# Second attention: its first half prepared inside the low-rank network, its projections made as 64-row products side by side in two banks

## The reference

```python
def _L0_ffn_ref(x, U1, V1, b1, U2, V2, b2):
    P = jnp.einsum('bsd,dr->bsr', x, U1)
    H = jax.nn.gelu(jnp.einsum('bsr,rf->bsf', P, V1) + b1)
    Q = jnp.einsum('bsf,fr->bsr', H, U2)
    return jnp.einsum('bsr,rd->bsd', Q, V2) + b2

def _L1_attn_ref(x, Wqkv, bqkv, Wr, br):
    xh = x.reshape(b, c, h, he).transpose(0, 2, 1, 3)        # 16 heads of 16
    qkv = jnp.einsum('bhce,ef->bhcf', xh, Wqkv) + bqkv       # one 16 x 48 weight for all heads
    q, k, v = jnp.split(qkv, 3, axis=-1)
    att = jnp.einsum('bhqe,bhke->bhqk', q, k) / jnp.sqrt(jnp.float32(he))
    mask = jnp.tril(jnp.ones((c, c), dtype=att.dtype), k=-1)
    att = jax.nn.softmax(att * mask, axis=-1)
    out = jnp.einsum('bhqk,bhke->bhqe', att, v)
    return out.transpose(0, 2, 1, 3).reshape(b, c, d) @ Wr + br
```

## Time and profile before

| | us |
|---|---|
| Median of 3 runs | 2801.05 |
| Lowest, highest | 2794.32, 2802.73 |
| Profiled execution | 2797.78 |
| its span, first to last instruction | 2796.0 |

### The profile page before, as it was taken

One profiled execution on the slowest core, in us unless ns is written; L12 is line 12 of the kernel. 1 busy time (PEld: TensorE's weight loads), 2 busy tenths in 40 slices (PEclk: granted clock), 3 DMA queues, 4 the chain that ended last, 5 costly groups with the idle time before them and its releaser, 6 DMA issues. The chain is left out here.

```text
span 2796.0 us, 75274 instructions
## 1 busy us (share of the span) xinstructions
PE 2615.3 (94%) x27044; PEld 1818.8 (65%) x27044; DVE 2280.6 (82%) x6931; ACT 2078.2 (74%) x3782; POOL 1811.9 (65%) x3152
## 2 busy tenths in 40 slices
PE   5999999999999999997889789999999999699999
PEld 3677777777777777775333257777777777466766
DVE  5999999999999999986655468888888888488998
ACT  4998899999998999895333257667677776478886
POOL 3767666777667766774421157677777767588885
PEclk8999999999999999999899889999999999899999
DMA  4334433444334433441000166655556664000001
GB/s 116 68 62 77 79 61 62 74 80 79 61 64 80 73 61 62 72 72 47 10 0 1 32 106 105 105 96 104 97 101 97 104 99 71 1 16 24 24 24 39
DMA packets 110387, 182.21 MB, mean 65 GB/s; under 512 B 27008, under 2 KB 96384, under 8 KB 97920
## 3 DMA queue, kind: packets, MB, share of 16 engines
q1 hardware_dynamic: 106560, 176.61, 34.7%
q10 hardware_dynamic: 3456, 0.79, 0.2%
HBM read 116.25 MB, written 60.29 MB: 63 GB/s over the span
## 5 line engine op out<-in xcount | busy, mean ns | idle before, releaser
L808 POOL TENSOR_TENSOR ratio_scores<-ratio_scores,ratio_max_cols 128x512 f32<-128x512 f32 (+3 forms) x1024 | 726.1, 726 | 319.3 <-DVE ratio_max_cols L718 316.9
L1328 DVE CUSTOM_DVE_ANT_0 zeroed_unused<-bank,zeroed_drop 128x512 bf16<-128x512 f32 (+3 forms) x1024 | 440.0, 484 | 121.1 <-PE bank L198 120.9
L198 PE MATMUL bank<-ratio_k_stack,ratio_q_stack 102*128 102x512 bf16 (+7 forms) x2048 | 506.3, 303 | 33.4 <-DVE ratio_max_cols L718 17.5
L718 DVE CUSTOM_DVE_ANT_0 ratio_scores<-bank,ratio_scores 128x512 f32<-128x512 f32 (+3 forms) x1024 | 472.4, 489 | 22.2
L1216 ACT ACTIVATE zeroed_prob<-bank 128x512 f32<-128x512 f32 x640 | 370.1, 593 | 161.2 <-PE bank L1103 160.3
L580 ACT ACTIVATE ratio_prob<-bank 128x512 f32<-128x512 f32 x640 | 378.4, 592 | 105.5 <-PE bank L494 102.7
L708 DVE TENSOR_TENSOR ratio_scores<-bank,ratio_inverse 128x512 f32<-128x512 f32 x640 | 435.9, 681 | 16.8 <-PE bank L198 9.6
L491 PE MATMUL bank<-const_f_sb,ratio_scores 128*128 128x128 f32 x2560 | 409.9, 274 | 0.9 <-ACT ratio_prob L580 0.9
L569 ACT ACTIVATE ratio_inverse<-bank 128x512 f32<-128x512 f32 x640 | 381.1, 596 | 12.7 <-PE bank L201 12.6
L573 ACT ACTIVATE ratio_inverse<-ratio_inverse 128x1024 f32<-128x1024 f32 x320 | 338.6, 1058 | 10.1
L1446 POOL TENSOR_SCALAR_AFFINE_SELECT zeroed_prob<-zeroed_prob 128x256 f32<-128x256 f32 (+1 forms) x640 | 227.7, 361 | 178.0 <-ACT zeroed_prob L1216 172.2
(11 more groups left out here) (178 smaller groups left out, 5412.6 us busy)
## 6 DMA issues: line engine op xcount, KB each, us to landing
ratio_q_stack<-ratio_parts_q SPq DMA_DIRECT2D x186, 128.0 KB
ratio_k_stack<-ratio_parts_k SPq DMA_DIRECT2D x186, 128.0 KB
zeroed_q_stack<-zeroed_parts_q SPq DMA_DIRECT2D x186, 128.0 KB, 4.7
zeroed_k_stack<-zeroed_parts_k SPq DMA_DIRECT2D x186, 128.0 KB, 7.7
ratio_parts_q<-ratio_parts SPq DMA_DIRECT2D x96, 128.0 KB
ratio_parts_k<-ratio_parts SPq DMA_DIRECT2D x96, 128.0 KB
zeroed_parts_q<-zeroed_parts SPq DMA_DIRECT2D x96, 128.0 KB
zeroed_parts_k<-zeroed_parts SPq DMA_DIRECT2D x96, 128.0 KB
```

The costliest lines, as they stand in the source:

```text
L198: i = e.matmul(bank[:, off:off + w], qs[0:rows, s, hh, ib * P:(ib + 1) * P], ks[0:rows, s, hh, 0:w], start=(k == 0), stop=mask is None, sk ...
L718: i = e.tensor_tensor_reduce(seg, dot_banks[n % 2][:, at], seg, 1.0, 0.0, ALU.mult, ALU.max, mx[:, pair % M_BUFS, c:c + 1])
L808: i = e.tensor_tensor(seg, seg, mx[:, pair % M_BUFS, c:c + 1].to_broadcast([P, w]), ALU.subtract)
L1328: i = e.tensor_tensor_reduce(unused[:, n % 2, at], bank[:, at], drop[:, L - (ib + 1) * P:L], 1.0, 0.0, ALU.add, ALU.max, mx[:, pair % FOLD ...
```

## The change

The first half's preparation (half 0) moves into rows 10 to 14 of the low-rank network (`START_AT`, `START_XN`, `START_MEMSETS`), with its constants and its gathers; what the stages share is now allocated around both (`ZeroedStart`), and the ternary weights' work tiles lie in the stacks' memory. ACT takes the Ln and Exp of the layer norm there, between two Gelus. Half 1 is prepared from slots 0 and 2.

A projection is now four products of 64 rows and 64 columns: heads 0 to 3 in `prep_bank`, heads 4 to 7 in `o_bank` (in the low-rank network in `post_bank`), the two halves of the 512 positions one below the other. ACT and DVE read each bank with an instruction of its own. So a projection waits until ACT has copied the last group out of `o_bank`, and every attend waits until the projections before it are read (`two_banks`). Values likewise: eight products for four. q and k are projected in slots 13 and 16; all three later steps follow one, two and three slots behind; the attends stand at 10, 12, 13 instead of 9, 11, 13, that is in slots 18, 20, 21 and 8, 10, 11. A side's parts are written by 6 DMAs with pieces of 256 elements (512 bytes) instead of 3 with 512.

```diff
 FOLD_PROBS = 12
-Z_ATTEND_AT = (9, 11, 13)
+Z_ATTEND_AT = (10, 12, 13)
...
-Z_ROOT_AT, Z_XN_AT, Z_TURN_AT, Z_VALUES_AT, Z_SUFFIX_AT = 0, (3, 6), (6, 9), 3, 19
-Z_SPLIT_AT, Z_REST_AT, Z_MID_AT, Z_LO_AT = (11, 15), (12, 16), (13, 17), (14, 18)
+Z_ROOT_AT, Z_XN_AT, Z_TURN_AT, Z_VALUES_AT, Z_SUFFIX_AT, Z_SPLIT_AT = 0, (3, 6), (6, 9), 3, 19, (13, 16)
+Z_REST_LAG, Z_MID_LAG, Z_LO_LAG = 1, 2, 3
+QUARTER = HALF // 2
 GROUPS_FROM, ROW_STEPS = ZEROED_LAG + 18, (71, 81, 91, 101)
-
-Z_SECOND_AT, Z_SECOND_REST_AT, Z_SECOND_MID_AT, Z_SECOND_LO_AT = (1, 5), (2, 6), (3, 7), (4, 8)
...
+def split_at(n, halves):
+
+    half, at = divmod(n, HALF_UNITS)
+    if n in Z_SECOND_AT:
+        return 1, Z_SECOND_AT.index(n)
+    if half >= 0 and at in Z_SPLIT_AT and half + 2 < halves:
+        return half + 2, Z_SPLIT_AT.index(at)
     return None, None
 
...
-            def project(half, side):
+            def project(half, side, n):
+
                 q.wait_ge(w.sem, w.loaded)
                 q.wait_ge(s["prep_read"], prep[sides[side], half] - 1)
-                e.matmul(prep_bank[:, :], w.w_in[:, side, :], xnT[:, half % 2, :], start=True, stop=True).then_inc(s["prep_filled"])
-
-            def values(half):
+                q.wait_ge(s["o_group"], groups_before(n))
+                for bank, heads in quarters:
+                    for k in range(2):
+                        i = e.matmul(bank[k * 64:(k + 1) * 64, 0:L // 2], w.w_in[heads, side, heads],
+                                     xnT[heads, half % 2, k * L // 2:(k + 1) * L // 2], start=True, stop=True, skip_group_check=True)
+                i.then_inc(s["prep_filled"])
+
+            def values(half, n):
                 q.wait_ge(s["prep_read"], prep["v", half] - 1)
+                q.wait_ge(s["o_group"], groups_before(n))
                 for t in range(T):
-                    i = e.matmul(prep_bank[:, t * P:(t + 1) * P], xnT[:, half % 2, t * P:(t + 1) * P], w.w_in[:, 2, :],
-                                 start=True, stop=True)
+                    for bank, heads in quarters:
+                        i = e.matmul(bank[:, t * 64:(t + 1) * 64], xnT[heads, half % 2, t * P:(t + 1) * P], w.w_in[heads, 2, heads],
+                                     start=True, stop=True, skip_group_check=True)
                 i.then_inc(s["prep_filled"])
 
...
                     q.wait_ge(s["prep_read"], prep["v", g // 2])
                     q.wait_ge(s["o_group"], g)
+                    q.wait_ge(s["prep_read"], two_banks(n))
                     attend(e, g, part, o_bank, values_ones, prob, FOLD_PROBS, STACKS).then_inc(s["attended"])
...
-                q.wait_ge(s[f"parts_{sides[side]}"], 48 * half)
-                e.activation(parts[:, side, 0, :], prep_bank[:, :], ACT.Identity, bias=w.bias_qk[:, side:side + 1]).then_inc(s["hi"])
+                q.wait_ge(s[f"parts_{sides[side]}"], 96 * half)
+                for k, (bank, _) in enumerate(quarters):
+                    i = e.activation(parts[:, side, 0, k * L // 2:(k + 1) * L // 2], bank[:, 0:L // 2], ACT.Identity,
+                                     bias=w.bias_qk[:, side:side + 1])
+                i.then_inc(s["hi"])
 
...
+                split_half, side = split_at(n, halves)
+                if split_half is not None:
+                    split(split_half, side)
+                split_half, side = split_at(n - Z_MID_LAG, halves)
+                if split_half is not None:
+                    second_part(split_half, side)
...
-                e.scalar_tensor_tensor(out=rest[:, :], in0=prep_bank[:, :], scalar=w.bias_qk[:, side:side + 1],
-                                       in1=parts[:, side, 0, :], op0=ALU.add, op1=ALU.subtract).then_inc(s["prep_read"])
+                for k, (bank, _) in enumerate(quarters):
+                    cols = slice(k * L // 2, (k + 1) * L // 2)
+                    i = e.scalar_tensor_tensor(out=rest[:, cols], in0=bank[:, 0:L // 2], scalar=w.bias_qk[:, side:side + 1],
+                                               in1=parts[:, side, 0, cols], op0=ALU.add, op1=ALU.subtract)
+                i.then_inc(s["prep_read"])
...
-                                parts[:, side, part, :]).then_inc(s[f"parts_{sides[side]}"], 16)
+                    for k in range(2):
+                        to = part_dram[side][half % 2][part][:, :, k * L // 2:(k + 1) * L // 2]
+                        e.dma_start(to.rearrange("d (m h) t -> h d m t", m=2),
+                                    parts[k * 64:(k + 1) * 64, side, part, :]).then_inc(s[f"parts_{sides[side]}"], 16)
...
+
+    slot = lambda b, f: b * FC + f
+    START_ROOT, START_XN = slot(11, 0), (slot(11, 5), slot(12, 4))
+    START_AT = dict(zip(START_STEPS, (slot(11, 7), slot(12, 7), slot(13, 1), slot(13, 7), slot(14, 1), slot(14, 7))))
+    START_TAILS = slot(14, 4)
+    START_MEMSETS = slot(10, 5), slot(11, 1), slot(11, 5), slot(11, 7), slot(12, 1), slot(12, 5)
...
-        w_pos = sb("ternary_w_positive", [P, 2, n_w])
-        w_neg = sb("ternary_w_negative", [P, 2, n_w])
+
+        flat = lambda stack: stack[:, :, :, :].rearrange("p s h t -> p (s h t)").bitcast(F32)
+        w_loaded = flat(start.qs)[:, 0:2 * n_w].rearrange("p (k n) -> p k n", k=2)
+        w_pos = flat(start.ks)[:, 0:2 * n_w].rearrange("p (k n) -> p k n", k=2)
+        w_neg = [flat(stack)[:, 2 * n_w:3 * n_w] for stack in (start.qs, start.ks)]
...
+            def start_project(side, n):
+
+                q.wait_ge(zeroed.sem, zeroed.loaded)
+                q.wait_ge(s["prep_read"], prep[sides[side], 0] - 1)
+                q.wait_ge(s["post_read"], post((n - OUT_AT[1] - 1) // FC - 1, 1))
+                for bank, heads in quarters:
+                    for k in range(2):
+                        i = e.matmul(bank[k * 64:(k + 1) * 64, 0:L // 2], zeroed.w_in[heads, side, heads],
+                                     start.xnT[heads, 0, k * L // 2:(k + 1) * L // 2], start=True, stop=True, skip_group_check=True)
+                i.then_inc(s["prep_filled"])
...
+                q.wait_ge(s["prep_read"], two_banks(slot(b + 1, OUT_AT[pair])))
...
+            def start_root():
+                e.preload_act_table_set("natural_log_exp_and_others")
+                e.activation(net.rstd[:, 0:T], net.mean_var[:, 0:T, 1], ACT.Ln, bias=net.eps_ln[:, :]).then_inc(zs["log_var"])
+                q.wait_ge(zs["log_var"], 1)
+                e.activation(net.rstd[:, 0:T], net.rstd[:, 0:T], ACT.Exp, scale=-0.5).then_inc(zs["rstd"])
+
...
+                if late[0] in ("q", "k"):
+                    side = side_of(late[0])
+                    q.wait_ge(zs["hi"], side + 1)
+                    q.wait_ge(zs["lo"], side)
+                    for k, (bank, _) in enumerate(quarters):
+                        cols = slice(k * L // 2, (k + 1) * L // 2)
+                        i = e.scalar_tensor_tensor(out=start.rest[:, cols], in0=bank[:, 0:L // 2], scalar=zeroed.bias_qk[:, side:side + 1],
+                                                   in1=start.parts[:, side, 0, cols], op0=ALU.add, op1=ALU.subtract)
...
+                q.wait_ge(zs["hi"], side + 1)
+                q.wait_ge(zs["lo"], side + 1)
+                for part in range(3):
+                    for k in range(2):
+                        to = start.part_dram[side][0][part][:, :, k * L // 2:(k + 1) * L // 2]
+                        e.dma_start(to.rearrange("d (m h) t -> h d m t", m=2),
+                                    start.parts[k * 64:(k + 1) * 64, side, part, :]).then_inc(zs[f"parts_{sides[side]}"], 16)
+            for heads, sem in ((slice(0, GROUP), zs["gathered_first"]), (slice(GROUP, HALF), zs["gathered0"])):
```

More of the change, by code:

```diff
@@ L1015, in zeroed_attention @@
+def zeroed_attention(net, w, start):
     nc, B, L, D, T = net.nc, net.B, net.L, net.D, net.T
@@ L1358, in prepare @@
                     values(half + 1)
-                if half == 0 and at in Z_SECOND_REST_AT:
-                    split(1, Z_SECOND_REST_AT.index(at))
                 if half % 2 == 0 and half + 2 < halves:
@@ L1377, in dve @@
                     maxima(n)
+                split_half, side = split_at(n - Z_REST_LAG, halves)
+                if split_half is not None:
+                    split(split_half, side)
                 if half < halves:
@@ L1470, in pool @@
                     split_maxima(pair - 1)
+                split_half, side = split_at(n - Z_LO_LAG, halves)
+                if split_half is not None:
+                    split(split_half, side)
                 if half < halves:
```

268 lines of the change are left out of this document (177 added, 91 removed).

## The result

| | us |
|---|---|
| Before, median of 4 runs | 2798.77 (2794.32 to 2802.73) |
| After, median of 4 runs | 2924.86 (2922.58 to 2931.66) |
| Ratio | 1.0455, 95% interval 1.043 to 1.048 |
| Profiled execution after | 2923.84, span 2922.1 |

The change costs 126 us. The forecast was 2845, 44 us over the 2801.05 that it started from, with a range of its own of 2825 to 2865. The direction and the mechanism came, the size did not.

What follows compares the result with a forecast made beforehand. PE was taken to bound the steady part, with DVE just hidden behind it. 2797.8 - 25 (start) + 70 (steady halves) = 2842.8 us, forecast as 2845 since the runs' median lies 3.3 above that execution; range 2825 to 2865.

Steps and rivals of the forecast that it cites:

- The start: Half 0's preparation inside the low-rank network and half 1's after it: -25 us, bounds -20 and -34.
- The mechanism: Steady half: PE waits 2.2 us before attend 0 for DVE's rest of k, which waits for POOL's low part of q.
- The size of the half, +2.4 us: Net cost of each steady half, paid in halves 1 to 29: 29 x 2.4 = +70 us.
- Attend 0 starts at S+8.2: Slot 18, S being the half's dots(12): attend 0 starts at S+8.2, not S+5.1; dots(19) comes 2.7 us later.
- Values: taken 0: Eight products for four in v's projection: between half of 0.95 us and twice, taken as 0.
- Slots 2 to 12: -0.3: These slots lose q's projection: worth nothing in halves with a turn of x, about 0.6 us otherwise, mean -0.3.
- The clock, taken as 1.00: PE's clock in the steady halves: the forecast added no cost for a slower clock behind the 2.2 us wait.
- rival C: PE's clock slows behind waits from about 3 us on, some 2 us more per half: 2900 us, chance 0.06.
- my own sign: Listed as showing the forecast wrong: PE's clock below 1.00 between 1650 and 2400.
- Transfers: 0: Writes and gathers of k's parts in steady halves: cost 0, some 3 us of cover stay; without it 1 to 3.
- Rivals A: POOL less behind; DVE's own work alone sets attend 0 at S+7.1, +38 us: 2814 us, chance 0.22.
- B: No wait at attend 0; PE saves 2 x 0.4 us per half, -23: 2753 us, chance 0.14.

Runs made afterwards that it cites:

- Experiment 1: Changed kernel's start only; later halves project q, k and v as before the change, attends at 9, 11, 13: 2776.22 us, ratio 0.9919 to the kernel before.
- experiment 3: Changed kernel with a second place for k's rest from half 2 on: 2855.00 us, ratio 1.0199 to the kernel before.
- experiment 10: Experiment 1 with v alone made as in the changed kernel, eight products of 64 rows in two banks: 2786.64 us, ratio 0.9951 to the kernel before.
- experiment 2: Experiment 1 (one bank) with the changed kernel's late slots, attends at 10, 12, 13 and projections at 13 and 16: 2834.69 us, ratio 1.0123.
- experiments 5: Changed kernel with q's low part ahead of the split of the maxima on POOL in slot 16: 2892.50 us, ratio 1.0324 to the kernel before.
- 7: Changed kernel with both a second place for k's rest and q's low part ahead of the split of the maxima: 2898.54 us, ratio 1.0349.
- Experiment 4: Changed kernel with the first block of shifted products made 34 times over ahead of attend 0 in slot 18: 2897.48 us, ratio 1.0345.
- experiment 8: Second place for k's rest and q's low part ahead of the maxima split, plus 18 repeated products ahead of attend 0: 2875.91 us, ratio 1.0270.

## Why the prediction was right or wrong

**The start: -25, measured -23.** Its steps held: the network grew by 5.0 us (I had 6, bounds 4 to 10), dots(0) came at 1581.7 (1582.6), dots(20) at 1615.6 (1614). Experiment 1 shows that it stands by itself.

**The mechanism: right.** One PE gap per half ahead of attend 0, released by DVE's rest of k, which waited for POOL's low part of q. The wait was forecast as 2.2 us and is mostly 2.4. That the two are so near is in part luck: PE comes to attend 0 at S+6.7 where I had 6.0, and DVE lets it go at S+9.1 where I had 8.2, so both ends were wrong the same way. The trace agrees with the page "TensorEngine Tiling (Array Packing)" of the Trainium skill, section PSUM Bottleneck, that the emptying of PSUM may become the bottleneck: in experiment 3, with POOL out of the chain, attend 0 still waits 1.1 us for the engine that empties the banks.

**The size of the half, +2.4 us: the step that failed.** At full clock a half costs 3.66 more (27.14 and 28.67, mean 27.90, against the 24.24 of 23.69 and 24.79), so 29 x 3.66 = 106 instead of 70. Two terms were mis-sized and make up nearly all of the 1.26 a half:
- "Attend 0 starts at S+8.2": S+9.1, and so 16.6 us from dots(12) to dots(22) where I had 15.7, 0.9 too little. q's projection waits for ACT's copy of the group and starts at S+1.0, not 0.7; its middle part stands behind two exponentials and ends at S+4.5, not 3.95; the split of the maxima takes 1.5 us, not 1.34, and begins when the mask of slot 15 ends, S+5.3, where I had 4.8. I added up durations and took each queue as free at the right moment.
- "Values: taken 0": 0.28 a half, by experiment 10.

"Slots 2 to 12: -0.3" was nearly right for what it counted, the loss of q's projection: experiment 2, with values as before, has -0.04 in the halves with a turn of x and -0.36 in the others, mean -0.2. In the kernel after, which has the dearer values in the same slots, it is +0.28 (12.04 for 11.76) and -0.05.

**The clock, taken as 1.00: the other step.** It stood in rival C, "from about 3 us on", with a chance of 6 in 100. Waits of 1.8 to 2.4 us were enough in 16 of 29 halves, and 1.57 in some halves of experiments 5 and 7. So by my own sign (a clock below 1.00 between 1650 and 2400) rival C came about on top of the forecast, at shorter waits than it named. Experiment 4 prices it at 37.6 us (some 31 without the odd half), experiment 8 at 32.6 in the halves of its kernel. That "about 3" came from one gap of 9.3 us, in which the only window I read lay 3 us behind its begin; no row showed that shorter gaps are safe, and I should have kept half of the 2 us per half in the sum.

**Transfers: 0, right.** No dot product of 1700 to 2400 waits for a gather.

The two steps make 106 + 38 = 144 of the 144.8 us; up to 7 of the 38 belong to the odd half, which neither step explains. Rivals A and B had less wait than the forecast; there was more.
